# Causal mask of the maximum products: added on VectorE in the pass that takes the maximum, in place of f16 mask products on TensorE

## The chip, the cores and the metric

The kernel runs on one core of a Trainium2 chip. The metric is the device time of one execution in microseconds; lower is better. TensorE (PE in the profile, PEld for its weight loads) multiplies, VectorE (DVE), ScalarE (ACT) and GpSimd (POOL) work beside it, SyncE (SP) issues most transfers.

## The reference

Input is x of 4 x 1024 x 256 in float32. Six layers follow one another, each on the layer-normalised x and each added to x: a gated feed-forward (256 to 768), attention without a mask, the same feed-forward again, a feed-forward with GELU (256 to 1024), causal attention, and the GELU feed-forward again. The change concerns the causal attention:

```python
q = _rope(q)
k = _rope(k)                                             # 16 heads of 16, sequence 1024
add_mask = jnp.where(i[:, None] >= i[None, :], 0.0, NEG) # NEG = -10000
scores = jnp.einsum('bhqd,bhkd->bhqk', q, k) * SCALE + add_mask
attn = jax.nn.softmax(scores, axis=-1)
out = jnp.einsum('bhqk,bhkd->bhqd', attn, v)
```

The softmax subtracts the largest masked score of each query before it takes the exponent.

## The kernel before

Both attentions come from one function, `attention_stage` (from L1241), called with causal False, then True. It works in 16 iterations, one for each batch and group of four heads. The four heads stand as two pairs of two slots; the slots use the upper and the lower 64 rows of TensorE's array, so that two matmuls of one pair run side by side. Keys and queries are held as parts (48 rows a slot), and two more rows carry the negated maximum of each query, so that the score matmul of the second kind subtracts it by itself.

Each iteration computes the score products twice. The first time (`max_unit` on TensorE, L1383) they are taken with queries on partitions, into `s_max` in PSUM, only for the maximum, which VectorE takes along the keys (`max_unit` on VectorE, L1545, a `tensor_reduce`) into `maxes`; L1552 negates and joins them, TensorE transposes the result (L1399), ScalarE copies it (L1490), GpSimd splits it into two parts (L1608, L1610), and SP's transfers put them beside the queries. The second time (`scores`, L1423) they are taken with keys on partitions into `s_exp`, a ring of three banks; ScalarE takes the exponent (L1524), and `values` (L1447) multiplies by the values into `o_ps`, which ScalarE copies out (L1503) once for each half of 512 queries.

A unit is one piece of the maximum work: a tile of 128 queries (qt) against up to 512 keys (kc), for one pair where there are over 256 keys, for both where there are fewer. `s_max` has two buffers (MBUFS = 2): TensorE writes unit a when VectorE has done unit a - 2. A step is a tile of 128 keys against up to 512 queries; it has two slots of work on TensorE, each with the scores of one pair, then the units that the plan has put there, then half of the values of the step before.

The order is written out ahead of time by the class `Plan`. It gives a step a cost of its columns plus 32 and a unit a cost of its keys times pairs plus 48, and spreads the units of the next iteration evenly over the steps by these costs, ahead by a fixed slack. Engines run their queues in order. The causal stage has two programs, `general` and `below`, and a number computed on the chip (`outweighed`) chooses: if no score can outweigh the mask, `below` leaves out all products above the diagonal. For the data given it is `below` that runs. It has 12 steps and 20 units an iteration. The units, with their keys and the query tile: 0 (tile 0, 128 keys, both pairs), 1 (tile 1, 256, both), 2 and 3 (tile 2, 384), 4 and 5 (tile 3, 512), 6 and 7 (tile 4, the first 512), 8 (tile 4, the other 128, both), 9 and 10 (tile 5, 512), 11 (256, both), 12 and 13 (tile 6, 512), 14 and 15 (384), 16 and 17 (tile 7, 512), 18 and 19 (tile 7, the other 512). Units 0 to 5, 8, 11, 14, 15, 18 and 19 reach the diagonal: 12 of 20. The plan's steps carry in their slots, in order: step 0 units 4 and 5; step 1 nothing and 6; step 2 units 7 and 8; step 3 nothing; step 4 units 9 and 10; step 5 units 11 and 12; step 6 unit 13, then 14 with 15; step 7 units 16 and 17; step 8 units 18 and 19; then units 0 to 3 of the iteration after next, in steps 9 to 11. Before the first iteration stands an opening of all 20 units and four more, with no other work in it.

The mask is added by matmuls into the same PSUM bank (`mask_pair`, L1354). The query mask `mask_q` is a table of 128 x 2048 in f16, -10000 right of the diagonal and 0 elsewhere; a slice of it is a mask. In `below` only the last 128 columns of a unit can be masked, and since a slot has only 64 rows of the array, two matmuls do it: L1359 multiplies one half of an identity by one half of the table, and L1360 a rolled identity (`swap16`) by the rolled table (`mask_q_swapped`), which brings the other 64 rows. So each pair of a unit at the diagonal costs four short matmuls. The mask of the second product (`mask_k`) is done in the same way, with L1423's products, and stays.

Every fourth iteration from the sixth on, VectorE takes a reciprocal of the last batch's sums (L1122), in step 6, ahead of unit 13.

Of the kernel before, what the change touches and what calls it, by code (L numbers as in the profile page):

```python
# [20 lines left out]
F16 = mybir.dt.float16  # L21
I32 = mybir.dt.int32
ALU = mybir.AluOpType
ACT = mybir.ActivationFunctionType
AX = mybir.AxisListType

P = 128
B, S, D = 4, 1024, 256
# [9 lines left out]
LAMBDA = 0.5  # L38
CLIP = 1e-9
# [12 lines left out]
HALF = P // 2  # L52
# [935 lines left out]
MBUFS = 2  # L988
# [262 lines left out]
def attention_stage(nc, E, name, causal):  # L1251

    UROWS = GH * 4
    with ExitStack() as ctx:
# [12 lines left out]
        maxes = sb("maxes", [P, KC, 2, PAIRS, 4, KC], F32)  # L1267
# [7 lines left out]
        s_max = ps("s_max", [P, MBUFS, 2, 512])  # L1275
        s_exp = ps("s_exp", [P, RING, 512])
# [73 lines left out]
        def _(pe):  # L1350
            def path(plan):
                NS, NU = plan.NS, plan.NU

                def mask_pair(out, table, swapped, at, cols, slot):  # L1354

                    if not plan.below:
                        return pe.matmul(out, E.ident16[:, :], table[:, at:at + cols], start=False, stop=True)
                    rows = slice(slot * HALF, (slot + 1) * HALF)
                    pe.matmul(out, E.ident16[rows, :], table[rows, at:at + cols], start=False, stop=False)  # L1359
                    return pe.matmul(out, E.swap16[rows, :], swapped[rows, :], start=False, stop=True)  # L1360
# [5 lines left out]
                def max_unit(it, a):  # L1366
# [10 lines left out]
                    qc, pairs, qt, kc, keys = plan.units[a]  # L1377
                    masked = plan.masked and kc * 512 + keys - 1 > qt * P
                    for pr in range(pairs.start, pairs.stop):
                        begin = (pr - pairs.start) * keys  # L1380
                        for slot in range(2):
                            rows = slice(slot * HALF, (slot + 1) * HALF - MROWS)
                            mm = pe.matmul(s_max[:, a % MBUFS, slot, begin:begin + keys], q_st[it.set][rows, qc, pr, (qt - 4 * qc) * P:(qt - 4 * qc + 1) * P],  # L1383
                                           k_st[it.set][rows, pr, kc * 512:kc * 512 + keys], start=True, stop=not masked)
                        if masked:
                            k0 = keys - P if plan.below else 0
                            at = S + kc * 512 + k0 - qt * P
                            for slot in range(2):
                                mm = mask_pair(s_max[:, a % MBUFS, slot, begin + k0:begin + keys], E.mask_q, E.mask_q_swapped,
                                               at, keys - k0, slot)  # L1390
# [19 lines left out]
                def scores(it, step, j, first):  # L1410
                    qc, kt, q0 = plan.steps[step]
                    pr, slot = j // 2, j % 2
# [12 lines left out]
                    if masked:  # L1425
                        q1 = q0 + P if plan.below else 512
                        at = S + qc * 512 + q0 - kt * P
                        mm = mask_pair(s_exp[:, plan.bank[place], q0:q1], E.mask_k, E.mask_k_swapped, at, q1 - q0, slot)
# [105 lines left out]
        def _(v):  # L1534
# [3 lines left out]
            def path(plan):  # L1538
                NS, NU = plan.NS, plan.NU

                def max_unit(it, a):
                    v.wait_ge(s["sa_ready"], it.n(NU, a + 1))
                    qc, pairs, qt, kc, keys = plan.units[a]
                    banks = s_max[:, a % MBUFS, :, 0:(pairs.stop - pairs.start) * keys].rearrange("p s (a k) -> p s a k", k=keys)
                    v.tensor_reduce(maxes[:, qc, :, pairs, qt - 4 * qc, kc], banks, AX.X, ALU.max).then_inc(s["max_done"], 1)  # L1545
# [218 lines left out]
def program(nc, io, out_dram):  # L1764
    E = Env()
    E.semaphores = []
    with ExitStack() as ctx:
# [61 lines left out]
        with ExitStack() as layer:  # L1829
# [11 lines left out]
            E.mask_q_swapped = layer.enter_context(nc.sbuf_tensor("mask_q_swapped", [P, P], F16))  # L1841
# [3 lines left out]
            def scale_small(v, s):  # L1845
# [16 lines left out]
                            (E.mask_q_swapped[:, :], io["mask_q_swapped"]), (E.mask_k_swapped[:, :], io["mask_k_swapped"]),  # L1862
# [19 lines left out]
def shape_constants():  # L1882
# [18 lines left out]
        "mask_q_swapped": np.ascontiguousarray(np.roll(mask_q[:, S:S + P], HALF, axis=0)),  # L1901
# [41 lines left out]
```

## Time and profile before

| | |
|---|---|
| time, median of 3 runs | 2249.92 us (2249.15 to 2250.74) |
| time of the profiled execution | 2249.36 us |
| its span, first to last instruction | 2247.6 us |
| TensorE, VectorE, ScalarE, GpSimd busy | 92%, 71%, 60%, 22% |
| causal attention stage, from the first to the last score product | about 1479 to 2005 us |

A line of groups names the line of the kernel, the engine, the operation, the tile written and the tiles read, the shapes, the count, the busy time and mean duration of one in ns, and the idle time ahead of them with what ended it. Names carry the program's tiles, not their buffer numbers. The modelled ends of pipelined matmuls overlap, so the starts in a timeline, and not the busy time, tell what a matmul costs. A timeline merges equal instructions that follow one another; its first column is the first start, its second the length of the merged row.

### The profile page before, as it was taken

Reading aid. Unit: us, or ns where it says so; the run is one execution under the profiler, and the core shown is the slowest. Engines: PE = TensorE matmul, PEld = TensorE weight load, DVE = VectorE, ACT = ScalarE, POOL = GpSimd, SP = SyncE. Lnnn points to the kernel's source line nnn. Section 1 sums busy time; section 2 is a strip of 40 time slices with the busy share of each in tenths; the row PEclk is TensorE's granted clock in tenths of the full one; section 3 lists DMA queues with packets and bytes.
Section 4 is the critical chain, followed back from the end, with each engine's and each line's share of the span. In section 5 each row is a group of like instructions: output and inputs, shape, how many; then the busy total and the mean of one; then the engine's idle time right before and its main releaser. Section 6 shows DMA issues by size and latency. Waiting matters only on the chain. (4 is left out here: it accounts for less than half of the span.)

```text
span 2247.6 us, 45906 instructions
## 1 busy us (share of the span) xinstructions
PE 2077.4 (92%) x17861; PEld 1302.4 (58%) x17861; DVE 1602.0 (71%) x2067; ACT 1353.0 (60%) x2612; POOL 499.6 (22%) x566
## 2 busy tenths in 40 slices
PE   3998889999999999979969998959999999988998
PEld 3887733333333333358858887835555555557887
DVE  7776699999999999566764446867776777726333
ACT  3444358888888888824434445616766767652444
POOL 3001131211321321330012112952212212111110
PEclk9999979999999999999979999959999999999999
DMA  4003842343552543220020000963455446310000
GB/s 141 1 0 123 294 65 44 64 75 57 93 98 49 102 84 51 53 66 1 0 101 1 1 0 30 276 155 69 83 107 93 95 81 113 64 55 17 29 19 28
DMA packets 124522, 161.79 MB, mean 72 GB/s; under 512 B 54812, under 2 KB 78044, under 8 KB 124324
## 3 DMA queue, kind: packets, MB, share of 16 engines
q1 hardware_dynamic: 107252, 119.70, 24.8%
q0 software_dynamic: 16256, 37.82, 6.3%
q8 instruction: 131, 2.15, 0.4%
q10 hardware_dynamic: 816, 1.57, 0.2%
q14 instruction: 67, 0.55, 0.1%
HBM read 94.05 MB, written 63.70 MB: 70 GB/s over the span
## 5 line engine op out<-in xcount | busy, mean ns | idle before, releaser
L1545 DVE TENSOR_REDUCE att_maxes<-att_s_max 128x2 f32<-128x1024 f32 (+2 forms) x832 | 974.0, 1183 | 160.8 <-PE att_s_max L1383 77.1
L1524 ACT ACTIVATE att_probs<-att_s_exp 128x512 f32<-128x512 f32 (+3 forms) x1792 | 887.9, 552 | 242.5 <-PE att_s_exp L1360 113.0
L1447 PE MATMUL att_o_ps<-att_probs,att_v_st 128*32 128x256 f32 (+1 forms) x6912 | 526.4, 376 | 15.0 <-ACT att_o_sb L1503 14.3
L1423 PE MATMUL att_s_exp<-att_q_st,att_k_st 64*128 64x512 f32 (+3 forms) x1120 | 283.7, 472 | 3.5 <-ACT att_probs L1524 2.1
L1447 PEld LDWEIGHTS att_o_ps<-att_probs,att_v_st 128*32 128x32 f32 x6912 | 138.5, 108 | 254.7 <-issue 139.8
L1423 PEld LDWEIGHTS att_s_exp<-att_q_st,att_k_st 64*128 64x128 f32 x1120 | 115.6, 183 | 214.4 <-ACT att_probs L1524 186.7
L1383 PE MATMUL att_s_max<-att_k_st,att_q_st 62*128 62x512 f32 (+2 forms) x1120 | 236.4, 398 | 2.0 <-DVE att_maxes L1545 1.9
L1383 PE MATMUL att_s_max<-operands_k_st,operands_q_st 62*128 62x512 f32 (+3 forms) x672 | 158.0, 449 | 36.6 <-DVE att_neg_max L1535 23.1
L1423 PE MATMUL att_s_exp<-operands_q_st,operands_k_st 64*128 64x512 f32 (+3 forms) x672 | 175.7, 478 | 2.1 <-ACT att_probs L1524 1.8
L1423 PEld LDWEIGHTS att_s_exp<-operands_q_st,operands_k_st 64*128 64x128 f32 x672 | 74.5, 187 | 129.6 <-ACT att_probs L1524 108.4
L1608 POOL TENSOR_TENSOR att_m_parts<-att_m_turned,att_zeros 32x128 fp32r<-32x128 f32 x64 | 28.9, 452 | 516.8 <-ACT att_m_turned L1490 377.5
L592 DVE TENSOR_TENSOR ffn1b_h_lo<-ffn1b_h,ffn1b_h_hi 128x512 fp32r<-128x512 f32 x64 | 44.5, 697 | 112.0 <-PE ffn1b_acc L135 100.2
L1383 PEld LDWEIGHTS att_s_max<-att_k_st,att_q_st 62*128 62x128 f32 x1120 | 115.7, 189 | 5.2 <-DVE att_maxes L1545 3.7
L592 DVE TENSOR_TENSOR ffn1a_h_lo<-ffn1a_h,ffn1a_h_hi 128x512 fp32r<-128x512 f32 x64 | 45.6, 713 | 100.4 <-PE ffn1a_acc L135 71.7
L1621 POOL DMA_DIRECT2D attention_rows<-att_o_sb x64 | 37.4, 585 | 356.9 <-ACT att_o_sb L1503 353.7
L1383 PEld LDWEIGHTS att_s_max<-operands_k_st,operands_q_st 62*128 62x128 f32 x672 | 73.8, 204 | 57.0 <-DVE att_maxes L1545 32.4
L503 ACT ACTIVATE ffn1a_h<-ffn1a_up,b 128x512 f32<-128x512 f32 x64 | 44.1, 689 | 99.3 <-PE ffn1a_up L135 99.3
L503 ACT ACTIVATE ffn1b_h<-ffn1b_up,b 128x512 f32<-128x512 f32 x64 | 44.1, 689 | 97.8 <-PE ffn1b_up L135 97.8
L132 PE MATMUL ffn1a_acc<-w_lo,ffn1a_h_hi 128*128 128x256 f32 x256 | 73.3, 286 | 7.4 <-DVE ffn1a_h_lo L592 7.3
L132 PE MATMUL ffn1b_acc<-w_lo,ffn1b_h_hi 128*128 128x256 f32 x256 | 73.1, 286 | 7.0 <-DVE ffn1b_h_lo L592 6.9
L135 PE MATMUL ffn1a_acc<-w_hi,ffn1a_h_hi 128*128 128x256 f32 x256 | 72.5, 283 | 0.0
L134 PE MATMUL ffn1a_acc<-w_hi,ffn1a_h_lo 128*128 128x256 f32 x256 | 72.5, 283 | 0.0
(319 smaller groups left out, 4152.8 us busy)
## 6 DMA issues: line engine op xcount, KB each, us to landing
attention_rows<-att_o_sb POOLq DMA_DIRECT2D x64, 256.0 KB, 4.0
att_q_st<-q_parts SPq DMA_DIRECT2D x240, 64.0 KB, 5.2
att_k_st<-k_parts SPq DMA_DIRECT2D x120, 128.0 KB, 4.6
output_wide<-attention_weights POOLq DMA_DIRECT2D x36, 256.0 KB, 5.4
operands_q_st<-q_parts SPq DMA_DIRECT2D x132, 64.0 KB, 5.1
operands_k_st<-k_parts SPq DMA_DIRECT2D x66, 128.0 KB, 4.7
q_parts<-qkv_parts SPq DMA_DIRECT2D x16, 512.0 KB, 4.4
k_parts<-qkv_parts SPq DMA_DIRECT2D x16, 512.0 KB, 3.9
```

The lines of the kernel that those rows point to most:

```text
L132: pe.matmul(out, left[0], right[1], start=first, stop=False, skip_group_check=skip)
L134: pe.matmul(out, left[1], right[0], start=first and whole == 1, stop=False, skip_group_check=skip)
L135: return pe.matmul(out, left[0], right[0], start=False, stop=last, skip_group_check=skip)
L503: act.activation(h[:, f % 2, :], up_ps[:, f % 2, 0, :], ACT.Gelu, bias=E.b1[:, f:f + 1]).then_inc(s["h_ready"], 1)
L592: v.tensor_tensor(h_parts[1][:, f % 2, :], h[:, f % 2, :], h_parts[0][:, f % 2, :].bitcast(F32), ALU.subtract).then_inc(s["h_lo"], 1)
L1383: mm = pe.matmul(s_max[:, a % MBUFS, slot, begin:begin + keys], q_st[it.set][rows, qc, pr, (qt - 4 * qc) * P:(qt - 4 * qc + 1) * P], k_st[ ...
L1423: mm = pe.matmul(s_exp[:, plan.bank[place], q0:512], k_st[it.set][rows, pr, kt * P:(kt + 1) * P], q_st[it.set][rows, qc, pr, q0:512], star ...
L1447: mm = pe.matmul(o_ps[j * VW:(j + 1) * VW, cols], v_st[:, it.par, kt, j, :], probs[:, step % 2, j, cols], start=kt == 0 and part == 0, sto ...
L1524: act.activation(probs[:, step % 2, j, q0:512], s_exp[:, plan.bank[place], q0:512], ACT.Exp, scale=1.0 if causal else 0.25).then_inc(s["ex ...
L1545: v.tensor_reduce(maxes[:, qc, :, pairs, qt - 4 * qc, kc], banks, AX.X, ALU.max).then_inc(s["max_done"], 1)
L1608: p.tensor_tensor(hi, m_turned[:, :], zeros[:, :], ALU.add).then_inc(s["m_step"], 1)
L1621: p.dma_start(E.o_dram[it.b, it.hg, :, qc * 512:(qc + 1) * 512], o_sb[:, qc, :]).then_inc(o_stored[qc], 16)
```

## The change

In `below`, TensorE adds no mask to the maximum products. VectorE does it: a unit that reaches the diagonal is no longer one `tensor_reduce` over both slots and all its pairs, but one `tensor_tensor_reduce` for each slot and pair (four for units 0, 1, 8 and 11, two for the other eight), over all keys of the unit. It adds the mask slice to the scores, writes the sum back to the same place in PSUM, and gives the maximum as a second output straight into `maxes`. Units that don't reach the diagonal are as before, and so are the `general` program and the mask of the second product. The rolled query table and its load are gone. The plan and its costs are the same.

```diff
+LOWEST = -3.0e38
...
-                def mask_pair(out, table, swapped, at, cols, slot):
+                def mask_scores(out, at, cols, slot):
 
                     if not plan.below:
-                        return pe.matmul(out, E.ident16[:, :], table[:, at:at + cols], start=False, stop=True)
+                        return pe.matmul(out, E.ident16[:, :], E.mask_k[:, at:at + cols], start=False, stop=True)
                     rows = slice(slot * HALF, (slot + 1) * HALF)
-                    pe.matmul(out, E.ident16[rows, :], table[rows, at:at + cols], start=False, stop=False)
-                    return pe.matmul(out, E.swap16[rows, :], swapped[rows, :], start=False, stop=True)
+                    pe.matmul(out, E.ident16[rows, :], E.mask_k[rows, at:at + cols], start=False, stop=False)
+                    return pe.matmul(out, E.swap16[rows, :], E.mask_k_swapped[rows, :], start=False, stop=True)
...
-                    masked = plan.masked and kc * 512 + keys - 1 > qt * P
+                    masked = plan.masked and not plan.below and kc * 512 + keys - 1 > qt * P
...
                         if masked:
-                            k0 = keys - P if plan.below else 0
-                            at = S + kc * 512 + k0 - qt * P
+                            at = S + kc * 512 - qt * P
                             for slot in range(2):
-                                mm = mask_pair(s_max[:, a % MBUFS, slot, begin + k0:begin + keys], E.mask_q, E.mask_q_swapped,
-                                               at, keys - k0, slot)
+                                mm = pe.matmul(s_max[:, a % MBUFS, slot, begin:begin + keys], E.ident16[:, :],
+                                               E.mask_q[:, at:at + keys], start=False, stop=True)
                     mm.then_inc(s["sa_ready"], 1)
...
                 def max_unit(it, a):
                     v.wait_ge(s["sa_ready"], it.n(NU, a + 1))
                     qc, pairs, qt, kc, keys = plan.units[a]
-                    banks = s_max[:, a % MBUFS, :, 0:(pairs.stop - pairs.start) * keys].rearrange("p s (a k) -> p s a k", k=keys)
-                    v.tensor_reduce(maxes[:, qc, :, pairs, qt - 4 * qc, kc], banks, AX.X, ALU.max).then_inc(s["max_done"], 1)
+                    if plan.below and kc * 512 + keys - 1 > qt * P:
+                        at = S + kc * 512 - qt * P
+                        for slot in range(2):
+                            for pr in range(pairs.start, pairs.stop):
+                                begin = (pr - pairs.start) * keys
+                                scores = s_max[:, a % MBUFS, slot, begin:begin + keys]
+                                ins = v.tensor_tensor_reduce(
+                                    out=scores, in0=scores, in1=E.mask_q[:, at:at + keys], scale=1.0, scalar=LOWEST,
+                                    op0=ALU.add, op1=ALU.max, accum_out=maxes[:, qc, slot, pr, qt - 4 * qc, kc:kc + 1])
+                        ins.then_inc(s["max_done"], 1)
+                    else:
+                        banks = s_max[:, a % MBUFS, :, 0:(pairs.stop - pairs.start) * keys].rearrange("p s (a k) -> p s a k", k=keys)
+                        v.tensor_reduce(maxes[:, qc, :, pairs, qt - 4 * qc, kc], banks, AX.X, ALU.max).then_inc(s["max_done"], 1)
...
-            E.mask_q_swapped = layer.enter_context(nc.sbuf_tensor("mask_q_swapped", [P, P], F16))
...
-                            (E.mask_q_swapped[:, :], io["mask_q_swapped"]), (E.mask_k_swapped[:, :], io["mask_k_swapped"]),
+                            (E.mask_k_swapped[:, :], io["mask_k_swapped"]),
```

## Rows read from the trace of the kernel before

**Rows 1.** The page: busy time, its share of the span, instructions.
```profile
PE 2077.4 (92%) x17861; PEld 1302.4 (58%) x17861; DVE 1602.0 (71%) x2067; ACT 1353.0 (60%) x2612; POOL 499.6 (22%) x566
```

**Rows 2.** Windows of the causal attention stage; after the engines, PEclk, DMA share, GB/s.
```profile
1479.40:1507.00 27.60, 22.94 (x150) 12.75 (x152) 24.34 (x25) 1.82 (x3) 19.16 (x18) 0.50 0.56 80
...
1514.00:1972.00 458.00, 448.29 (x5847) 233.93 (x5839) 332.44 (x324) 320.03 (x757) 96.72 (x134) 1.00 0.48 88
```

**Rows 3.** ScalarE timeline: copies of the second output half, three iterations.
```profile
1668.32 0.60 ACT L1503 ACTIVATE att_o_sb<-att_o_ps 128x512 f32<-128x512 f32 x1
...
1700.31 0.60 ACT L1503 ACTIVATE att_o_sb<-att_o_ps 128x512 f32<-128x512 f32 x1
...
1731.57 0.60 ACT L1503 ACTIVATE att_o_sb<-att_o_ps 128x512 f32<-128x512 f32 x1
```

**Rows 4.** Waits, 1507 to 1972: engine and line, us in all, times, longest.
```profile
PEld att_s_max L1383 <- DVE att_maxes L1545: 4.9, 15, 0.9
```

**Rows 5.** VectorE timeline, the stretch of units 9 to 17.
```profile
1708.13 10.62 DVE L1545 TENSOR_REDUCE att_maxes<-att_s_max 128x2 f32<-128x1024 f32 x9 [2.11 <-PE att_s_max L1383]
```

**Rows 6.** TensorE timeline, units 14 and 15 (384 keys each).
```profile
1713.96 0.34 PE L1383 MATMUL att_s_max<-att_k_st,att_q_st 62*128 62x384 f32 x2
1714.14 0.23 PE L1359 MATMUL att_s_max<-mask_q,ident 64*128 64x128 f16 x2
...
1714.45 0.45 PE L1383 MATMUL att_s_max<-att_k_st,att_q_st 62*128 62x384 f32 x2
```

**Rows 7.** TensorE timeline, unit 8 (128 keys, two pairs).
```profile
1704.74 0.24 PE L1359 MATMUL att_s_max<-mask_q,ident 64*128 64x128 f16 x2
...
1704.84 0.31 PE L1383 MATMUL att_s_max<-att_k_st,att_q_st 62*128 62x128 f32 x2
```

**Rows 8.** VectorE timeline, the reciprocal of iteration 5.
```profile
1681.08 0.94 DVE L1122 RECIPROCAL output_weights<-output_sums 128x128 f32<-128x128 f32 x1
```

**Rows 9.** Groups by line and form, 1507 to 1972: count, busy us, mean ns, idle before.
```profile
L1545 DVE TENSOR_REDUCE att_maxes<-att_s_max 128x2 f32<-128x1024 f32 x179 | 218.5, 1225 | 69.7 <-PE att_s_max L1383 50.7 <-PE att_s_max L1360 16.0
...
L1359 PE MATMUL att_s_max<-mask_q,ident 64*128 64x128 f16 x470 | 62.3, 230 | 0.0
...
L1360 PE MATMUL att_s_max<-mask_q_swapped,swap 64*128 64x128 f16 x470 | 59.4, 218 | 0.0
...
L1545 DVE TENSOR_REDUCE att_maxes<-att_s_max 128x2 f32<-128x768 f32 x60 | 56.1, 956 | 36.1 <-PE att_s_max L1360 34.9
...
L1545 DVE TENSOR_REDUCE att_maxes<-att_s_max 128x4 f32<-128x512 f32 x29 | 20.1, 693 | 5.9 <-PE att_s_max L1360 4.3
```

**Rows 10.** TensorE timeline, two units: start us, us, line, operands, count.
```profile
1715.86 0.39 PE L1383 MATMUL att_s_max<-att_k_st,att_q_st 62*128 62x512 f32 x2
1716.18 0.64 PE L1447 MATMUL att_o_ps<-att_probs,att_v_st 128*32 128x256 f32 x8
...
1718.41 0.49 PE L1383 MATMUL att_s_max<-att_k_st,att_q_st 62*128 62x512 f32 x2
1718.74 0.24 PE L1359 MATMUL att_s_max<-mask_q,ident 64*128 64x128 f16 x2
...
1718.96 0.64 PE L1447 MATMUL att_o_ps<-att_probs,att_v_st 128*32 128x256 f32 x8
```

**Rows 11.** DMA issues of the page: KB each, us to landing.
```profile
att_q_st<-q_parts SPq DMA_DIRECT2D x240, 64.0 KB, 5.2
```

**Rows 12.** VectorE timeline, in the opening.
```profile
1480.68 0.69 DVE L1545 TENSOR_REDUCE att_maxes<-att_s_max 128x4 f32<-128x512 f32 x1 [1.77 <-PE att_s_max L1360]
...
1487.42 0.17 DVE L1552 TENSOR_REDUCE att_neg_max<-att_maxes 128x16 f32<-128x16 f32 x1
1487.51 5.59 DVE L1545 TENSOR_REDUCE att_maxes<-att_s_max 128x2 f32<-128x1024 f32 x5
1493.46 4.35 DVE L1545 TENSOR_REDUCE att_maxes<-att_s_max 128x4 f32<-128x1024 f32 x4 [0.36 <-PE att_s_max L1360]
```

**Rows 13.** Line 939, sums before: ns min/median/max, first and last start.
```profile
L939 DVE TENSOR_TENSOR qkv_with_cos<-qkv_qk,cos x16: 1214/1216/1225, 1385.8 to 1458.2; 128x1024 f32<-128x1024 f32 x16
```

More of the change, by code:

```diff
@@ L1427, in scores @@
                         at = S + qc * 512 + q0 - kt * P
-                        mm = mask_pair(s_exp[:, plan.bank[place], q0:q1], E.mask_k, E.mask_k_swapped, at, q1 - q0, slot)
+                        mm = mask_scores(s_exp[:, plan.bank[place], q0:q1], at, q1 - q0, slot)
                     mm.then_inc(s["st_ready"], 1)
@@ L1900, in shape_constants @@
         "mask_k": mask_k,
-        "mask_q_swapped": np.ascontiguousarray(np.roll(mask_q[:, S:S + P], HALF, axis=0)),
         "mask_k_swapped": np.ascontiguousarray(np.roll(mask_k[:, S:S + P], HALF, axis=0)),
```

## The prediction

> **What bounds the kernel now.** I read the page's head first: TensorE is busy 92% of the span, VectorE 71% [rows 1]. An average over stages says nothing of this change, which touches only the causal attention stage, so next I cut that stage out by windows [rows 2]. It has an opening, 1479 to 1507 us at half clock, in which the maxima of the first iteration are taken with nothing beside them; there VectorE is the busier (24.34 of 27.60 us). From 1507 on scores, exponents and values run; from 1514 to 1972 TensorE is busy 448 of 458 us at full clock, VectorE 332, ScalarE 320. The last 34 us have no maxima left.
>
> The 16 iterations have a period: two copies of the same output half are 31.26 us apart [rows 3]. 15 such periods carry maxima. Is TensorE's stream really what sets 31.26? The waits say so, nearly: its score weights wait for a maximum only 4.9 us in 15 waits [rows 4]. But VectorE is close behind. In one stretch of each iteration (the four full-width steps of the second query half) it does nine units in 10.62 us without a row of idle time [rows 5], and the place where it holds TensorE up is there: the scores of unit 15 follow those of unit 14 after 0.49 us; 0.18 of it is unit 14's own product [rows 6] and 0.10 its mask group [rows 7], which leaves 0.21 of waiting for unit 13's maximum. The proof that this stretch is tight: where a reciprocal of 0.94 us stands on VectorE, in three iterations, the period is 1700.31 - 1668.32 = 31.99, 0.73 longer [rows 3, 8]. So TensorE bounds the period with some tenths of a microsecond of play, and anything added on VectorE in that stretch comes through once the play is used up.
>
> **What goes.** The maximum product has 512 mask matmuls of each kind, straight and swapped, 1024 / 16 = 64 a period [rows 9]; four (two slots, straight and swapped) make a group, 16 groups a period. Their rows of 0.22 to 0.24 us overlap, so busy time is no price; starts are. Ahead of values, an unmasked pair of 512 columns gives way after 1716.18 - 1715.86 = 0.32 us, a masked one after 1718.96 - 1718.41 = 0.55 [rows 10]: 0.215 a group, taken over the period's other places too. Where another score pair follows, the group takes 1704.84 - 1704.74 = 0.10 [rows 7], and some of that is cover for the next weights, so I take 0.09. Ten groups are of the first kind, five of the second, one is followed by the other product (0.15 between these two): 2.15 + 0.45 + 0.15 = 2.75 us a period off TensorE's stream. The mask on the exponent product stays. The load of the swapped table (32 KB of DMA on SP's queue, behind work of the previous stage) goes too. I cost it at nothing: the feed-forward stage before the projections hides it, and bare it could be worth at most about the 5.2 us in which a transfer of 64 KB lands [rows 11].
>
> **What comes on VectorE.** A period has 20 units, 12 of them on the diagonal. Those 12 reduces become 32 pieces (8 query tiles x 2 pairs x 2 slots), one each of 128 to 512 elements; the elements are the same. Price of a piece:
> - Per element: a reduce has 693 ns for 512 and 1225 for 1024 elements [rows 9], 1.04 ns each. A two-source instruction that reads PSUM takes 1216 ns for 1024 [rows 13], the same, so I take 1.04 for the new one, also with its result going back to PSUM, which no row shows.
> - Per instruction: alone it shows 0.16 us beside its elements, but reduces back to back overlap: four starts in 4.35 us with the last 0.95 long [rows 12] are 1.13 apart at 1024 elements, so 0.07 is what one adds. 20 more a period: 1.4 us.
> - The second output, the maximum itself, c: not in this trace. Below, 0. Above, if the pieces don't overlap (0.09 more) and the accumulated value comes out in a short instruction of its own at full length (0.17 - 0.02, the small reduce of 16 elements [rows 12]): 0.24. I take 0.07, that small instruction overlapped (1487.42 to 1487.51 less its elements [rows 12]), because all short VectorE work in this stream overlaps so. 32 x 0.07 = 2.2 us a period.
>
> The Trainium skill (VectorE: DVE Perf Modes, "Two Vector instructions with no wait between them") says that an operation which also writes its accumulator counts as two instructions. That bears on c and on nothing else: by it c is not 0 and the time is 2218 rather than 2211. No run here shows it yet. The same page ("The TRN2 errata") charges 120 cycles per instruction from PSUM, an estimate of 0.125 us where our rows show 0.07; by it the time is some 4 us more, and the rows decide.
>
> **How it lands.** VectorE's demand goes from 21.1 us (18432 elements, 20 reduces, two small ones) to 24.7 of the period: below TensorE. What counts is the tight stretch. Unit 11 becomes 4 x (0.27 + 0.07 + 0.07) = 1.63 us for 1.13, +0.50 ahead of unit 13. Some is absorbed: back to back the nine units would take 7 x 1.13 + 2 x 0.87 + 0.09 = 9.7 us, so their 10.62 hold 0.9 of play, and half of it, 0.44 to 0.46, lies ahead of unit 13 (unit 11 can start 0.20 earlier with no mask matmuls to wait for, and there are small gaps behind it). VectorE is then 0.04 late at unit 13's end, while TensorE comes to unit 15 by 0.30 + 0.07 earlier. The wait of 0.21 becomes 0.61. Units 14 and 15 are +0.21 each, and units 16 to 19 start later behind them, but by then TensorE is held back by the same wait and their buffers free in time (0.2 to 0.8 us left). The pieces of units 0, 1 and 8 lie where VectorE has idle time around each unit; so do those of 2 to 5, 18 and 19 at this price. The period: 31.26 - 2.75 + 0.40 = 28.91; with the steps unrounded 28.94, 2.32 less. The three reciprocals still add about 0.74 each, as now.
>
> ScalarE waits or is fed by TensorE throughout (320 of 458 us) and comes to 22 us in 28.9; its ring waits and the output copy's wait of 0.3 are chains that begin at TensorE and move with it. GpSimd and the transfers have room of the same kind. The clock is at its upper level through the stretch [rows 2], TensorE stays over 95% busy, so I leave it.
>
> The opening has no cover: VectorE sets it. Until the first exponent product it does 40 pieces where it did 14 reduces: 26 x 0.07 + 40 x 0.07 = 4.6 us more, less 2.0 of idle time behind the first reduce (3.3 in the window [rows 2], less 1.3 ahead of its start at 1480.68 [rows 12]), and 0.5 for mask matmuls that the first and the last unit no longer wait for: +2.1 us, at half clock.
>
> Sum: 15 x 2.32 = 34.8, less 1.0 for units 0 to 3, which the last period doesn't take: 33.8; less 2.1: **31.7 us**. The profiled execution takes 2249.36 us (its span is 2247.6), so 2217.7; the median of the runs lies 0.56 above it: **2218**.
>
> **The other cases.**
> - *No price for the second output* (c = 0): the period is 28.66, the opening 0.7 shorter: 2211. With what I took within a few hundredths (c to 0.1) it makes one case, 2210 to 2223.
> - *Pieces hand over one after another* (c about 0.155: the accumulated value must wait for the piece to end). VectorE needs 27.4 of the period and now the waits at units 13, 15 and 1 add up: 29.46, opening +5.5: 2229. For it: the value is known only at a piece's end. Near it in time is that the mask groups hid weight loads, and only their own 0.10 each comes back: 1.6 a period, with a shorter wait: 2235. Against that: an unmasked pair hands over in 0.32 without them [rows 10].
> - *VectorE becomes the bound* (slower). If a piece costs over c = 0.21, the maxima of units 11, 14, 15 keep TensorE waiting in the tight stretch and unit 5's before the turn: at 0.24 the period is 31.44 and the opening 9 longer: 2262. For it: the reciprocal shows that 0.94 on VectorE comes out as 0.73 there [rows 3, 8], and 32 pieces are many. Against: it needs every overlap lost that the rows show.
> - *Half rate.* If the new instruction takes two cycles an element, 10240 elements more a period at 1.04 ns put VectorE at 33 to 34 us a period: about 2310. The Trainium skill (Vector Engine (DVE) Microarchitecture Reference, "Points that are easy to get wrong") states halved throughput for one instruction family with two SBUF sources that are not bf16. Here one source is PSUM, and the two-source row that reads PSUM goes at full rate [rows 13].
> - *The change doesn't do what it says*, no mask matmuls gone or the slower program path chosen: the diff excludes it but for a hundredth: 2250.
>
> **Numbers.** The forecast's case 0.60, handing over and the smaller gain together 0.21, VectorE as bound 0.14, half rate 0.04, nothing 0.01. The three runs differ by 0.07%, and about 0.2% (4.5 us) is what a measurement of this kernel can tell from no change. Faster gets 0.60 + 0.20, same 0.05 (the passage near c = 0.2, at 2247), slower 0.15. The range takes the first two cases whole and the point where it turns: 2207 to 2252; the likeliest case's own is 2210 to 2223.
>
> **What would show it.** In the changed profile: no rows of the straight and swapped query mask, 512 new VectorE rows of about 0.29, 0.43, 0.56 and 0.69 us, perhaps each with a short row behind it; starts of pieces of 256 elements 0.41 apart (0.34 if c is 0, 0.50 if they hand over, 0.58 if VectorE bounds). Output copies 28.9 apart. Values 0.32 behind an unmasked or masked unit alike. A wait of 0.6 for the maximum at unit 15, and the first exponent product at about 1509 instead of 1507. I am wrong if the copies stay 30.5 or more apart, if the score weights wait for maxima in most units, or if the starts after a score pair don't close up to 0.32.

## The result, and the profile after

The changed kernel takes 2234.86 us in the median of five runs (2227.49 to 2236.60), the kernel before 2249.92 (2249.15 to 2250.74, five runs): a ratio of 0.9919, 95% interval 0.9901 to 0.9937. The profiled execution took 2236.03 us, its span is 2234.2; 13.4 us of span are gone. The page's line of busy time, then the window of full running; both answer to [rows 1, 2].

```profile
PE 2052.5 (92%) x16837; PEld 1272.8 (57%) x16837; DVE 1641.4 (73%) x2899; ACT 1352.3 (61%) x2612; POOL 500.7 (22%) x566
```

```profile
1514.00:1972.00 458.00, 441.32 (x5125) 216.48 (x5125) 368.73 (x1080) 330.34 (x791) 101.95 (x140) 0.98 0.50 89
```

The 1024 query-mask matmuls are gone (17861 less 16837). TensorE is still the busy engine; VectorE has 369 of 458 us where it had 332. The ScalarE timeline gives the period, as in [rows 3]:

```profile
1667.84 0.60 ACT L1503 ACTIVATE att_o_sb<-att_o_ps 128x512 f32<-128x512 f32 x1
...
1698.21 0.60 ACT L1503 ACTIVATE att_o_sb<-att_o_ps 128x512 f32<-128x512 f32 x1
...
1727.89 0.60 ACT L1503 ACTIVATE att_o_sb<-att_o_ps 128x512 f32<-128x512 f32 x1
```

The plain period is 29.68 (1727.89 - 1698.21) for 31.26, and 30.37 where the reciprocal stands: 1.58 less, not 2.32. The span divides as follows (from the timelines of both kernels; the copy is the one that closes the first or the last iteration):

| stretch | before | after | difference |
|---|---|---|---|
| start to the first maximum product | 1479.5 | 1481.5 | +2.0 |
| opening, to the first exponent product | 27.55 | 27.69 | +0.1 |
| to the first closing copy | 36.19 | 39.98 | +3.8 |
| to the last closing copy | 462.83 | 442.69 | -20.1 |
| to the end | 241.55 | 242.39 | +0.8 |

Two things were not in my sum: a loss of 3.8 us in the first iteration, and 2.0 us ahead of a stage that the change doesn't touch. I come back to both in the last experiment (The spread) and in the sum at equal clock.

**VectorE does what was foreseen.** The groups by form of VectorE, 1549 to 1960 us (count, busy us, mean ns), and the timeline of unit 11 (four pieces of 256):

```profile
L1550 DVE CUSTOM_DVE_ANT_0 att_s_max<-att_s_max,mask_q 128x512 f32<-128x512 f32 x110 | 73.5, 716 | 2.4 <-PE att_s_max L1384 0.5
L1550 DVE DVE_READ_ACCUMULATOR2_ANT att_maxes<- 128x1 f32 x434 | 61.9, 143 | 0.0
L1550 DVE CUSTOM_DVE_ANT_0 att_s_max<-att_s_max,mask_q 128x384 f32<-128x384 f32 x108 | 57.7, 587 | 21.5 <-PE att_s_max L1384 21.5
L1550 DVE CUSTOM_DVE_ANT_0 att_s_max<-att_s_max,mask_q 128x256 f32<-128x256 f32 x108 | 42.5, 457 | 0.4
L1550 DVE CUSTOM_DVE_ANT_0 att_s_max<-att_s_max,mask_q 128x128 f32<-128x128 f32 x108 | 28.1, 323 | 0.3
```

```profile
1708.44 0.14 DVE L1550 DVE_READ_ACCUMULATOR2_ANT att_maxes<- 128x1 f32 x1
1708.44 0.47 DVE L1550 CUSTOM_DVE_ANT_0 att_s_max<-att_s_max,mask_q 128x256 f32<-128x256 f32 x1
1708.83 0.14 DVE L1550 DVE_READ_ACCUMULATOR2_ANT att_maxes<- 128x1 f32 x1
1708.83 0.47 DVE L1550 CUSTOM_DVE_ANT_0 att_s_max<-att_s_max,mask_q 128x256 f32<-128x256 f32 x1
...
1709.21 0.47 DVE L1550 CUSTOM_DVE_ANT_0 att_s_max<-att_s_max,mask_q 128x256 f32<-128x256 f32 x1
```

Each piece has a second row, the read of its accumulator, of 0.143 us. But that row begins together with the next piece, so its length is no price. Starts are: 0.38 apart for 256 elements, of which 0.27 are the elements and 0.07 the instruction; c, the price of the second output, is the rest: 0.04 to 0.05. The elements go at full rate, back into PSUM too (716 - 457 = 259 ns for 256). The Trainium skill (VectorE: DVE Perf Modes, "Two Vector instructions with no wait between them") counts such an operation as two instructions, and by its rule neither would be held here, since all tiles begin at partition 0; the rows agree: there are two, and the row at 1708.83 starts 0.08 before the one at 1708.44 ends.

**TensorE is where the sum was off.** Four rows of the TensorE timeline, first of the kernel before (unit 6, not at the diagonal), then of the kernel after (unit 2, whose mask is gone):

```profile
1702.00 0.48 PE L1383 MATMUL att_s_max<-att_k_st,att_q_st 62*128 62x512 f32 x2
1702.41 0.64 PE L1447 MATMUL att_o_ps<-att_probs,att_v_st 128*32 128x256 f32 x8
```

```profile
1715.94 0.49 PE L1384 MATMUL att_s_max<-att_k_st,att_q_st 62*128 62x512 f32 x2
1716.36 0.64 PE L1447 MATMUL att_o_ps<-att_probs,att_v_st 128*32 128x256 f32 x8
```

Behind an *exponent* product that is itself masked, an unmasked maximum pair gives way to values after 0.41 to 0.42, before and after alike. The 0.32 of [rows 10] is a pair behind an exponent product without a mask; the 0.55 beside it stands behind one with a mask. Like against like, 0.55 less 0.41, a group is worth 0.13 to 0.14, not 0.215. From start to start of the maximum products (medians over the periods), nine units got shorter: 0, 1 and 8 (two groups each) by 0.25, 0.31 and 0.26, and 2, 3, 5, 15, 18, 19 by 0.12 to 0.14. That is 12 groups for 1.60 us, and the period got 1.58 shorter. Four groups gave nothing:

- Unit 11, two groups. The values behind it wait for ScalarE's copy of the output half. TensorE timeline before, then after:

```profile
1709.19 0.43 PE L1447 MATMUL att_o_ps<-att_probs,att_v_st 128*32 128x128 f32 x8
...
1710.38 0.23 PE L1360 MATMUL att_s_max<-mask_q_swapped,swap 64*128 64x128 f16 x2
1710.58 0.64 PE L1447 MATMUL att_o_ps<-att_probs,att_v_st 128*32 128x256 f32 x8
```

```profile
1706.86 0.42 PE L1447 MATMUL att_o_ps<-att_probs,att_v_st 128*32 128x128 f32 x8
...
1707.55 0.40 PE L1384 MATMUL att_s_max<-att_k_st,att_q_st 62*128 62x256 f32 x4
1708.24 0.64 PE L1447 MATMUL att_o_ps<-att_probs,att_v_st 128*32 128x256 f32 x8 [0.30 <-ACT att_o_sb L1503]
```

  Values to values take 1.39 before and 1.38 after. The masks had filled a gap that the copy (0.63 us) makes in any case; now it shows as a wait of 0.30. So TensorE doesn't reach the units behind it earlier either: from unit 11 to unit 15 it takes 4.56 us in both kernels.
- Unit 14. Unit 15 waits for unit 13's maximum, as I had read; the mask group of 0.10 turned into 0.10 more of that wait. From unit 14 to unit 15 it takes 0.48 for 0.49, and from unit 13 to unit 15 1.73 in both. Here are the weight loads of unit 15 in the two kernels, before and after:

```profile
1714.45 0.19 PEld L1383 LDWEIGHTS att_s_max<-att_k_st,att_q_st 62*128 62x128 f32 x2 [0.19 <-DVE att_maxes L1545]
```

```profile
1712.11 0.19 PEld L1384 LDWEIGHTS att_s_max<-att_k_st,att_q_st 62*128 62x128 f32 x2 [0.52 <-DVE att_maxes L1556]
```

  The idle time of the weight loads grew from 0.19 to 0.52, but that is not what TensorE lost: what stood ahead of it before was the mask's weight load, and now it is that of unit 14's product, which ends earlier. By the starts of the products the wait is 0.48 - 0.18 = 0.30, where it was 0.21.
- Unit 4. Behind it stand the next slot's two exponent products. The second of them (1726.55) waits until ScalarE has taken an exponent and so freed a bank of the ring `s_exp`. TensorE timeline after:

```profile
1725.68 0.49 PE L1384 MATMUL att_s_max<-att_k_st,att_q_st 62*128 62x512 f32 x2
1726.00 0.40 PE L1423 MATMUL att_s_exp<-att_q_st,att_k_st 64*128 64x512 f32 x1
...
1726.31 0.22 PE L1361 MATMUL att_s_exp<-mask_k_swapped,swap 64*128 64x128 f16 x1
1726.55 0.50 PE L1423 MATMUL att_s_exp<-att_q_st,att_k_st 64*128 64x512 f32 x1
```

  From the first exponent product of the step to this one it takes 1.31 us before (1728.79 to 1730.10) and after (1725.24 to 1726.55), and unit 4 to unit 5 takes 0.88 in both.

### The profile page after: what moved, and what is told of

The parts are those of the page before. It is cut to its first block and busy times, and to the rows that moved or that the text cites. A ratio compares the mean times of both kernels' runs of the same rounds, so it can differ in the third digit from the quotient of the medians.

```text
span 2234.2 us, 44689 instructions
## 1 busy us (share of the span) xinstructions
PE 2052.5 (92%) x16837; PEld 1272.8 (57%) x16837; DVE 1641.4 (73%) x2899; ACT 1352.3 (61%) x2612; POOL 500.7 (22%) x566
## 5 line engine op out<-in xcount | busy, mean ns | idle before, releaser
L1556 DVE TENSOR_REDUCE att_maxes<-att_s_max 128x2 f32<-128x1024 f32 x640 | 773.7, 1223 | 77.7 <-PE att_s_max L1384 73.1
L1550 DVE CUSTOM_DVE_ANT_0 att_s_max<-att_s_max,mask_q 128x384 f32<-128x384 f32 (+3 forms) x512 | 237.2, 521 | 29.6 <-PE att_s_max L1384 26.9
L1384 PE MATMUL att_s_max<-att_k_st,att_q_st 62*128 62x512 f32 (+2 forms) x1120 | 231.6, 397 | 4.7 <-DVE att_maxes L1550 2.0
L1550 DVE DVE_READ_ACCUMULATOR2_ANT att_maxes<- 128x1 f32 x512 | 73.1, 143 | 0.0
```

The lines of the kernel that those rows point to most:

```text
L1550: ins = v.tensor_tensor_reduce(out=scores, in0=scores, in1=E.mask_q[:, at:at + keys], scale=1.0, scalar=LOWEST, op0=ALU.add, op1=ALU.max, ...
```

## The experiments

In all but the repeats of the change the choice is made by two small functions, in which `it.r` is the iteration and `a` the unit. The rolled table and its load are those of the kernel before. Against the changed kernel:

```diff
-masked = plan.masked and not plan.below and kc * 512 + keys - 1 > qt * P
+masked = plan.masked and kc * 512 + keys - 1 > qt * P and (not plan.below or tensor_masks(it, a))
...
-if plan.below and kc * 512 + keys - 1 > qt * P:
+if plan.below and kc * 512 + keys - 1 > qt * P and vector_masks(it, a):
```

What the five runs left open was, first, the period (is it TensorE's chains alone, or do the pieces on VectorE cost something?), and second, the spread: three of the five lie at 2235 to 2237, two at 2227 to 2228.

### The change again

No edit. 

> The changed kernel again, unchanged. Its five executions so far fall into two sets, 2227.5 to 2228.1 and 2234.9 to 2236.6 us, and the profiled one (2236.0) shows TensorE at half clock until about 1532 us, 24 us into the first iteration, where the kernel before left it 8 us in. Theory A (the opening without mask matmuls lets the clock stay down longer in some executions) expects the same two sets again, 2228 and 2236, 8 us apart, and a profiled run of the lower set with the clock back up near 1515 us. Theory B (the second set is something else, not the clock of this stage) expects two sets too, but the clock's rise at the same place in both.

Measured: 2226.55 us (2224.11 to 2233.15), ratio 0.9899 [0.9881, 0.9917]; period 29.66. Most of these runs fell near 2226, and the profiled one took 2224.11; it shows the early rise of the clock that theory A expected (The spread).

### The opening masked on TensorE, all else as changed

```diff
+def vector_masks(it, a):
+    return not (it.r == 0 or it.r == 1 and a < 4)
+def tensor_masks(it, a):
+    return (it.r == 0 or it.r == 1 and a < 4)
```

> The change, but the 24 units of the opening keep their mask matmuls on TensorE and their plain reduces. Theory A: the opening is as before (27.6 us), the clock rises 8 us into the first iteration as before, every execution is near 2227 us (2249.9 less 15 periods at 31.26 - 29.68 = 1.58, plus 0.8 that the last period has not to give) and the upper set is gone. Theory B: two sets as with the change, up to 2236.

Measured: 2227.31 (2226.83 to 2227.73, four runs), 0.9894 [0.9877, 0.9912], period 29.68. The opening takes 27.5 us here and 27.7 with the pieces: nearly equal. No run lies in the upper set, as theory A expected, but these are four runs, and a later one speaks against it (The spread).

### Only the opening on VectorE

```diff
+def vector_masks(it, a):
+    return (it.r == 0 or it.r == 1 and a < 4)
+def tensor_masks(it, a):
+    return not (it.r == 0 or it.r == 1 and a < 4)
```

> The reverse: only the 24 units of the opening have their mask on VectorE, all later units keep it on TensorE. The period is 31.26 as before. Theory A (clock): 2250 in some executions and about 2256 to 2258 in others, with the half clock lasting to about 1530 us. Theory B: 2250 in all, as the opening itself took 27.4 us in the change against 27.6 before.

Measured: 2250.81 (2246.22 to 2254.15, twelve runs), 1.0001 [0.9991, 1.0012], period 31.27. The whole gain lies in the periods. (The opening takes 27.7 us in the change; the 27.4 in the expectation was misread.) The runs don't fall into the two sets of theory A, and the profiled one has the early rise.

### Both masks

Both functions return True: masked scores get the mask on TensorE and once more in the pieces.

```diff
+def vector_masks(it, a):
+    return True
+def tensor_masks(it, a):
+    return True
```

> The pieces on VectorE and the mask matmuls on TensorE, both (the mask is added twice): VectorE's price alone, with nothing given back. Theory 1 (VectorE's pieces are cheap and mostly covered; each costs 0.07 + 0.045 beside its elements, 2.8 us a period): the wait for unit 13 grows by about 0.17, the period is 31.4 to 31.5, the time 2252 to 2256. Theory 2 (the pieces hold TensorE back in the tight stretch and this is where the expected 0.8 us a period went): the period is 32 or more, the time 2260 or more.

Measured: 2256.32 (2252.80 to 2260.72, ten runs), 1.0023 [1.0011, 1.0034]. ScalarE timeline:

```profile
1703.88 0.60 ACT L1512 ACTIVATE att_o_sb<-att_o_ps 128x512 f32<-128x512 f32 x1
...
1735.25 0.60 ACT L1512 ACTIVATE att_o_sb<-att_o_ps 128x512 f32<-128x512 f32 x1
```

The period is 31.37, 0.11 more than before, and unit 14 to 15 takes 0.59 for 0.49. The pieces by themselves do cost something at the one tight place, but a tenth of a microsecond. Of the 5.4 us by which this kernel is slower than the one before (2250.93 beside it), 2.4 are the opening (29.90 for 27.55) and some 2 the periods.

### No mask on the maximum products

The causal mask is left out altogether; the mask matmuls on the exponent product still run, on a table of zeros.

```diff
+def vector_masks(it, a):
+    return False
+def tensor_masks(it, a):
+    return False
...
-        "mask_k": mask_k,
+        "mask_k": np.zeros_like(mask_k),
...
-        "mask_k_swapped": np.ascontiguousarray(np.roll(mask_k[:, S:S + P], HALF, axis=0)),
+        "mask_k_swapped": np.zeros((P, P), dtype=np.float16),
```

> No mask on the maximum product at all, neither matmuls nor pieces (plain reduces, as in the kernel before), and the mask tables of the exponent product filled with zeros, its matmuls kept; so nothing is masked. TensorE is relieved as in the change and VectorE pays nothing. Theory 1 (the change's VectorE work is wholly covered; unit 15 waits for the reduce of unit 13, which takes 1.23 us from its own scores on, whatever the pieces do): the period is that of the change, 29.66 to 29.70. Theory 2 (the pieces cost part of the expected gain): 28.9 to 29.4. The time: 2226 by theory 1, 2216 to 2222 by theory 2.

Measured: 2227.57 (2224.25 to 2229.24), 0.9896 [0.9880, 0.9913]. The window, the copies, and then the waits of the score weights (1549 to 1960 us) of this kernel and of the changed one:

```profile
1514.00:1972.00 458.00, 440.29 (x5125) 215.78 (x5124) 329.44 (x325) 332.30 (x794) 102.25 (x141) 0.98 0.50 89
```

```profile
1694.33 0.60 ACT L1512 ACTIVATE att_o_sb<-att_o_ps 128x512 f32<-128x512 f32 x1
...
1724.00 0.60 ACT L1512 ACTIVATE att_o_sb<-att_o_ps 128x512 f32<-128x512 f32 x1
```

```profile
PEld att_s_max L1392 <- DVE att_maxes L1565: 9.3, 14, 1.2
```

```profile
PEld att_s_max L1384 <- DVE att_maxes L1556: 9.4, 14, 1.2
```

VectorE is relieved of 39 us, and the period stays at 29.67 with the same wait at unit 15. In the changed kernel the 32 pieces of a period cost nothing. This is the strongest of the runs: in this order of the units, no cheaper way of masking on VectorE would shorten the period. What is left at unit 15 is the wait for unit 13's plain reduce, which has no mask in any of the kernels. The opening does get shorter, from 27.7 to 24.8 us.

### Unit 11 alone on VectorE; all but unit 11 on VectorE

The opening is on TensorE in both; one profiled run each. For the first:

```diff
+def vector_masks(it, a):
+    return not (it.r == 0 or it.r == 1 and a < 4) and a == 11
+def tensor_masks(it, a):
+    return (it.r == 0 or it.r == 1 and a < 4) or a != 11
```

The second has, in effect, `a != 11` for `a == 11` and `a == 11` for `a != 11`.

> Only unit 11 has its mask on VectorE (in the 15 later iterations), all other units keep their mask matmuls. Theory 1 (behind unit 11 the values wait for ScalarE's copy of the first output half, so TensorE time saved there is waited away): values start 1.60 us after unit 11's place as before, the period stays 31.26. Theory 2: its two groups give back 0.26 to 0.3 us, the period is 31.0. The time: 2250 or 2246.

> The change, with the opening's units and unit 11 masked on TensorE again. Theory 1: the period stays at 29.68, for the two groups at unit 11 lie in the wait for ScalarE's copy, and the wait ahead of unit 15 is that for unit 13's own reduce. Theory 2 (unit 11's four pieces make unit 13 late): the wait ahead of unit 15 (0.30) gets shorter and the period is 29.4. The time: 2227 or 2223.

Measured: 2255.17 with a period of 31.30 (31.26 before), and 2236.59 with a period of 29.66 (29.68 in the change). Taking unit 11's two groups off TensorE gains nothing, and putting them back costs nothing: the copy's wait takes them up either way. The single times say nothing beyond that (The spread has what lengthened them).

### A new order of the units

Unit 15 waits because 13, 14 and 15 come within one step, and step 3 has none. This edit puts units 9 to 15 one to a slot, in slots 7 to 13:

```diff
+        if below:
+            moved = [(s, i) for s in range(7, 14) for i, x in enumerate(self.feed[s]) if x[1] == "unit" and 9 <= x[2] <= 15]
+            units = [self.feed[s].pop(0) for s, _ in moved]
...
+            for s, x in zip(range(7, 14), units):
+                self.feed[s].append(x)
```

> The change with the order of seven units shifted by hand: units 9 to 15, which lay in both slots of steps 4 and 5 and as one and two in step 6, lie one each in the second slot of step 3 and the six slots after it, so that VectorE begins unit 9 earlier and no slot has two units. Theory 1: the wait ahead of unit 15 (0.30 us) goes, the copy's wait in step 5 stays (1.38 us from the values ahead of it to those behind it), and the period is 29.40 to 29.50, the time 3 us under that of the change on the same chip. Theory 2 (VectorE or ScalarE holds the stretch elsewhere): the period stays at 29.68, or grows where unit 11 waits for unit 9.

Measured: 2220.05 (2214.70 to 2227.54), 0.9878 [0.9861, 0.9895]. ScalarE timeline, then the wait for maxima, 1507 to 1972 us:

```profile
1653.60 0.60 ACT L1519 ACTIVATE att_o_sb<-att_o_ps 128x512 f32<-128x512 f32 x1
...
1683.09 0.60 ACT L1519 ACTIVATE att_o_sb<-att_o_ps 128x512 f32<-128x512 f32 x1
...
1712.39 0.60 ACT L1519 ACTIVATE att_o_sb<-att_o_ps 128x512 f32<-128x512 f32 x1
```

```profile
PEld att_s_max L1399 <- DVE att_maxes L1566: 0.7, 3, 0.2
```

The plain period is 29.30 (1712.39 - 1683.09), somewhat below what was expected. The one with the reciprocal is 29.49 where it was 30.37: VectorE's 0.94 now mostly fits. The wait of 9.6 us (the changed kernel's in the same window) is down to 0.7.

Three kernels then ran together on one chip, to compare directly: the change once more, the change in the new order once more, and the new order by itself, with the edit of the order above and

```diff
+def vector_masks(it, a):
+    return False
+def tensor_masks(it, a):
+    return True
```

> The changed kernel unchanged, for a direct comparison with its new order on one chip. Period 29.67 us, 2226 to 2236 us, ratio near 0.990.

> The change together with units 9 to 15 one to a slot. Period 29.30 us (29.48 where the reciprocal is, 0.9 less than the change alone has there): the fourteen full periods save 12*0.37 + 3*0.90 = 7.1 us, so some 2219 to 2229, and below the change alone beside it by 6 to 8 us if what was gained in the one profile is the period; if it was the clock of that run, the two medians agree within 3 us.

> The new order alone, with the mask products of the kernel before on TensorE. Theory 1 (the order only takes away the wait of unit 15 for unit 13's maximum, 0.33 a period in the kernel before, 0.64 after the change, and gives 0.27 of it back elsewhere; a mask group is still worth 0.13): period 31.2, nothing gained, 2248. Theory 2 (the order is worth its 0.37 a period whatever the mask does): period 30.9, 2243.

| kernel | median us (range, runs) | ratio to before, 95% | period, with the reciprocal |
|---|---|---|---|
| before | 2250.79 (2247.07 to 2253.34, 17) | | 31.26, 31.99 |
| the change | 2234.17 (2224.76 to 2235.02, 6) | 0.9911 [0.9896, 0.9926] | 29.68, 30.37 |
| the change, new order | 2223.58 (2218.04 to 2225.56, 4) | 0.9868 [0.9854, 0.9882] | 29.33, 29.49 |
| new order alone | 2246.45 (2244.56 to 2251.08, 11) | 0.9983 [0.9974, 0.9991] | 31.23, 31.23 |

The change in the new order beats both kernels; its interval doesn't touch that of the change alone. It is 10.6 us faster than the change here, where 6 to 8 were expected. In the two profiles, which both have the late rise of the clock, 6.5 of 9.5 lie between the first and the last closing copy, as 11 x 0.35 + 3 x 0.88 = 6.5 says (the last of the fifteen periods has no maxima and gains nothing). Almost all the rest, 3.1, lies ahead of the first maximum product (1477.7 for 1480.8), where the code of the two is the same; I have no cause for it. The first theory held for the plain period of the order alone (31.23, 0.03 less). What it left out is the reciprocal, whose 0.73 went altogether: 11 x 0.03 + 3 x 0.76 = 2.6 us of the 4.3 measured, and 2.6 lies within the interval (2.0 to 5.9 us). So the order and the change help each other: the order is worth 0.03 a period without the change and 0.35 with it. The starts of the units in these two profiles say why. With the new order in both kernels, unit 14's group is worth 0.13 (1.31 to 1.18), since unit 15 no longer waits for a maximum. Unit 11's two are worth 0.17: 0.32 behind unit 11 (1.67 to 1.35), less 0.15 behind unit 12 (1.45 to 1.60), where the copy's wait now stands. In the old order all three were worth nothing.

### The spread

The kernels don't fall on one value: the kernel before spread over 10.7 us beside the first experiments (2245.9 to 2256.6 in 23 runs), the change over 12.5 (2224.11 to 2236.60 in 16 runs). The windows from 1514 to 1532 us of two profiles of the same changed kernel (first the one of 2236.03 us, then the one of 2224.11):

```profile
1514.00:1532.00 18.00, 18.00 (x129) 8.22 (x133) 9.06 (x22) 8.82 (x22) 3.93 (x4) 0.50 0.72 100
```

```profile
1514.00:1532.00 18.00, 17.33 (x199) 8.11 (x193) 16.09 (x48) 13.85 (x30) 3.92 (x4) 1.00 0.62 84
```

In the opening the granted clock is at its lower level (0.50, 1.2 GHz) in every profile, but it rises at about 1510 us in one and 1532 in the other, and from the first exponent product to the first closing copy it is 32.5 us in one and 40.0 in the other. With the mask matmuls in the periods the rise came at 1510 to 1518 in all five profiles (before, opening on VectorE, unit 11 alone, both, order alone). Without them (but for unit 11's in one) it came at 1508 to 1514 in three and at 1529 to 1533 in five. I had suspected the pieces in the opening. Against that: with the opening's masks on TensorE and all but unit 11 on VectorE behind it, the rise came at 1533 all the same, and with no pieces at all at 1529. What decides it is open. That kernels without the mask matmuls in the periods have a late rise more often would fit five of eight profiles against none of five, and isn't shown.

The last period, which has no maxima and the same work in all kernels, is a second such place. It takes 24.79 us in five profiles (the kernel before among them) and 25.99 in five (the change's first among them), but 27.15 with both masks and 30.0 with unit 11 alone and with the order alone. In the profile of unit 11 alone the granted clock is at the lower level there from 1982 to 1998 us; in that of the kernel before it is at the upper one throughout. This is 5.2 us of the 2255.17 of unit 11 alone; the 2236.59 of all but unit 11 has the late rise, at 1533.

## Why the prediction was right and where it was wrong

Faster it was, and 2234.86 lies in the range. But the case that I held likeliest, 2210 to 2223, is not what happened, and the range was wide (2207 to 2252). The place nearest in time, the smaller gain (1.6 a period, 2235), had its reason wrong in part and its number right by luck: it took 0.10 for each of 16 groups, where 12 gave 0.13 or so and 4 nothing, and the upper runs, near 2235, have a late rise of the clock in them that it did not count. By one of its own signs the prediction was wrong: behind masked exponent products the starts did not close up to 0.32, but to 0.41.

- **What bounds the kernel**: right. TensorE's stream sets the period before and after; without any mask work on VectorE it is the same.
- **What goes**, 2.75 us a period: the step that failed first. The group ahead of values was read off two rows that differ in two ways, a mask on the maximum product and one on the exponent product ahead of it. Like with like gives 0.13 where I took 0.215 for ten groups. And two waits were missing from the sum: at unit 11 (the copy) and unit 4 (the bank of `s_exp`) the mask matmuls filled time that is there without them. I had written that these chains begin at TensorE and move with it. They do move, but a wait of fixed length between two pieces of TensorE's work doesn't get shorter with the work inside it. Measured: 1.60, or 1.70 with unit 14's 0.10, which came off and turned into wait.
- **What comes on VectorE**: right. Pieces of 256 start 0.38 apart for 0.41, c = 0.045 for 0.07; full rate, also into PSUM; an accumulator row on top of the next piece.
- **How it lands**, +0.40: too much as well. I expected a wait of 0.61 at unit 15, so 0.18 + 0.61 = 0.79 from unit 14 to unit 15; it is 0.48, and the wait 0.30 for 0.21. TensorE was to come to unit 15 earlier by 0.37; as the copy took up unit 11's groups, it comes 0.10 earlier. Nor is VectorE late: the same 9.3 us of waits stand in the run without pieces, against 9.4. The two errors pull against each other: 2.75 - 0.40 = 2.35 forecast, 1.70 - 0.10 = 1.60 found.
- **The opening**: +2.1 foreseen, +0.1 measured. Timelines of the four kinds, first maximum product and first exponent product: before, after, no mask, both.

```profile
1479.48 0.48 PE L1383 MATMUL att_s_max<-operands_k_st,operands_q_st 62*128 62x128 f32 x2 [17.20 <-DVE att_neg_max L1535]
...
1507.03 0.77 PE L1423 MATMUL att_s_exp<-operands_q_st,operands_k_st 64*128 64x512 f32 x2
```

```profile
1481.45 1.01 PE L1384 MATMUL att_s_max<-operands_k_st,operands_q_st 62*128 62x128 f32 x6 [17.04 <-DVE att_neg_max L1535]
...
1509.14 0.63 PE L1423 MATMUL att_s_exp<-operands_q_st,operands_k_st 64*128 64x512 f32 x2
```

```profile
1480.64 1.23 PE L1392 MATMUL att_s_max<-operands_k_st,operands_q_st 62*128 62x128 f32 x8 [16.58 <-DVE att_neg_max L1544]
...
1505.44 0.63 PE L1432 MATMUL att_s_exp<-operands_q_st,operands_k_st 64*128 64x512 f32 x2
```

```profile
1480.05 0.48 PE L1392 MATMUL att_s_max<-operands_k_st,operands_q_st 62*128 62x128 f32 x2 [16.85 <-DVE att_neg_max L1544]
...
1509.95 0.78 PE L1432 MATMUL att_s_exp<-operands_q_st,operands_k_st 64*128 64x512 f32 x2
```

  That is 27.55, 27.69, 24.80 and 29.90 us. The pieces cost 2.9 (27.69 - 24.80), near my 4.6 - 2.0 = 2.6. The mask matmuls cost 2.75 there (27.55 - 24.80), where I had allowed 0.5 for two units only. At half clock a group is dearer: between the two pairs of the later unit 0, the products start 0.44 apart with the group (1502.59 and 1503.03) and 0.24 without (1504.69 and 1504.93), which is 0.20 a group, twice the 0.10 at full clock. That the rest comes from each unit at the diagonal handing over later to VectorE is my reading, not shown. The sign "first exponent product at about 1509" came true (1509.14) by luck: the stage began 2.0 us later.
- **The clock**: "so I leave it" was right for the periods and wrong for the first iteration. The sum at equal clock: fourteen periods of 1.6 (the first iteration's among them), and 0.6 of the last but one, are 23.0 us, less 0.1: 2226.5. That is what the lower runs of the change show. The profiled run lost 5.4 (3.8 + 1.6) by the late rise in the first iteration, 1.2 in the last period (25.99 for 24.79, with a stretch at lower clock in it), 2.0 ahead of the stage and 0.8 behind it: 2236.0.
- **The rivals**: hand-over, VectorE as bound, half rate and nothing at all are out, by the starts of the pieces, by the run without pieces, by 259 ns for 256 elements, and by the missing 1024 rows. (The half-rate case had a slip: 10240 elements at 1.04 ns on top of 24.7 are 35.4 us a period; 33 to 34 leaves the second output out.)

## What to carry to other kernels

To price a small instruction from two places of a timeline, compare places that are alike in what stands *before* them as well. Better still, take all places of a period, start to start. And for each place where work is taken off the bounding engine, ask whether a wait of fixed length (a copy, a ring buffer, another engine's own duration) spans it: there the work was free. When work that was taken off lay in such waits, the order of the work may be worth changing next; the same order was worth 0.03 us a period before the change and 0.35 after. And read a wait by the starts on both sides of it: the idle time of the weight loads grew by 0.33 us where TensorE lost 0.10.

## What the runs showed that I had not expected

- A reduce with a second output has a row of 0.143 us of its own for the accumulator, yet adds only 0.045 us from start to start.
- The same kernel raises TensorE's clock from the lower to the upper level at 1510 us in one run and at 1532 in another, which is worth some 7 us, more than half of what the change gained in its profiled run.
- The stages ahead of the causal one do the same work in all the kernels, and yet its first maximum product starts between 1476.6 and 1482.2 us, 5.6 us apart. No run shows why.
